# A four-layer graph network on one core: the first basis products of the next edge tile are issued ahead of the first half of a tile's messages

## The reference

```python
def _L1_gnn_ref(node_feat, edge_sh, edge_inv, edge_weight_cutoff, Wk1, ..., Wv3, W_logit, W_out, edge_src, edge_dst):
    x_src = node_feat[edge_src]
    def f(W1, W2, W3):
        tp = (x_src[:, :, None] * edge_sh[:, None, :]).reshape(n_edges, d * s)   # 64 features x 8 components
        out1 = jnp.concatenate([x_src, tp], axis=-1)                             # 576 columns
        out2 = _mlp(edge_inv, W1, W2, W3)
        return out1 * out2
    ...
    alpha = exp / z[edge_dst]                     # softmax weights over the edges of a destination, 4 heads
    edge_v = f(Wv1, Wv2, Wv3)
    edge_v = edge_v.reshape(n_edges, H, F // H) * jnp.sqrt(jax.nn.relu(alpha))[:, :, None]
    node_out = jax.ops.segment_sum(edge_v.reshape(n_edges, F), edge_dst, num_segments=n_nodes)
    return node_out @ W_out
```

## Time and profile before

| | us |
|---|---|
| median of 3 runs (lowest, highest) | 4221.5 (4217.95, 4222.28) |
| the profiled execution's own time | 4220.62 |
| its span in the trace | 4218.8 |
| DVE busy in the span | 3706.1 |
| PE busy in the span | 3078.8 |

### The profile page before, as it was taken

The page is one execution under the profiler, slowest core; times in us unless marked ns, Lnnn a source line. Parts: engine busy times, 40 slices in busy tenths (PEclk is TensorE's granted clock), DMA queues, the critical chain, the costliest instruction groups (busy, mean ns, idle before and its releaser), DMA issues. The chain is left out here.

```text
span 4218.8 us, 129416 instructions
## 1 busy us (share of the span) xinstructions
PE 3078.8 (73%) x53233; PEld 1918.5 (45%) x53233; DVE 3706.1 (88%) x5487; ACT 1777.2 (42%) x3388; POOL 1850.4 (44%) x3678
## 2 busy tenths in 40 slices
PE   5566556466388888888883699999999995166166
PEld 2111111212156566666662577777777774122122
DVE  8999999799778888888788888888888885898898
ACT  6999988477222232333231222222222221085086
POOL 0100455100376676777672466666666665000000
PEclk9889887677699999999997899999999997598599
DMA  4863899766255555555551233333333332554554
GB/s 162 307 269 147 301 362 353 264 205 210 71 139 143 138 152 146 145 148 147 149 144 54 66 103 102 102 103 104 103 101 102 103 104 83 190 198 181 190 182 175
DMA packets 412793, 680.07 MB, mean 161 GB/s; under 512 B 75244, under 2 KB 353068, under 8 KB 400560
## 3 DMA queue, kind: packets, MB, share of 16 engines
q1 hardware_dynamic: 336736, 559.22, 40.0%
q0 software_dynamic: 39568, 78.78, 6.9%
q10 hardware_dynamic: 35904, 33.79, 2.7%
HBM read 399.92 MB, written 271.65 MB: 159 GB/s over the span
## 5 line engine op out<-in xcount | busy, mean ns | idle before, releaser
L734 POOL DMA_INDIRECT arena<-h_table,srci x808 | 773.7, 958 | 315.5 <-issue 205.8
L830 PE MATMUL banks<-arena 128*128 128x500 bf16 x1440 | 428.8, 431 | 278.9 <-DVE arena L1496 219.7
L1901 DVE TENSOR_TENSOR arena<-banks,arena 128x1024 f32<-128x1024 f32 x404 | 492.0, 1218 | 100.7 <-PE banks L1046 95.1
L1787 DVE TENSOR_TENSOR arena<-banks,arena 128x1024 f32<-128x1024 f32 x404 | 491.8, 1217 | 68.5 <-PE banks L937 63.9
L1909 DVE TENSOR_TENSOR arena<-banks,arena 128x1024 f32<-128x1024 f32 x404 | 494.8, 1225 | 36.9 <-PE banks L1055 0.3
L1185 ACT ACTIVATE arena<-arena,h 128x128 bf16<-128x128 f16 x1440 | 454.5, 386 | 81.3 <-DVE arena L1509 41.4
L1055 PE MATMUL banks<-arena 64*64 64x256 f32 x6464 | 432.8, 383 | 50.0 <-DVE arena L1909 50.0
L948 PE MATMUL banks<-arena 64*64 64x128 f32 x12928 | 437.4, 274 | 0.0
L1074 PE MATMUL banks<-arena 64*64 64x128 f32 x12928 | 435.8, 272 | 0.3 <-DVE arena L1909 0.3
L1484 DVE TENSOR_SCALAR arena<-arena,agg 128x500 bf16<-128x500 f16 x1440 | 410.4, 345 | 0.2
L830 PEld LDWEIGHTS banks<-arena 128*128 128x128 bf16 x1440 | 126.6, 104 | 579.7 <-DVE arena L1484 438.8
(11 more groups left out here) (297 smaller groups left out, 5768.0 us busy)
## 6 DMA issues: line engine op xcount, KB each, us to landing
arena<-c_flat SPq DMA_DIRECT2D x75, 1562.5 KB, 6.8
slots<-arena SPq DMA_DIRECT2D x90, 1000.0 KB, 4.8
arena<-hs_dump SPq DMA_DIRECT2D x404, 128.0 KB
arena<-mask_rows SPq DMA_DIRECT2D x50, 781.2 KB, 4.3
arena<-in_edge_attr SPq DMA_DIRECT2D x202, 128.0 KB
arena<-placed SPq DMA_DIRECT2D x202, 128.0 KB
xs_dump<-arena SPq DMA_DIRECT2D x202, 128.0 KB
hs_dump<-arena SPq DMA_DIRECT2D x202, 128.0 KB
```

The source lines that it names most:

```text
L734: pool.indirect_dma_start(out=xs[par][:, k * D:(k + 1) * D], out_offset=None, in_=h_table, in_offset=bass.IndirectOffsetOnAxis(ap=srci[:, ...
L830: last = pe.matmul(ps[4 + r % 2][:, 0:BW], row_hot[r][:, k * P:(k + 1) * P], col_hot[r][:, k * BW:(k + 1) * BW], start=k == 0, stop=k == K ...
L1787: V.tensor_tensor(bt[h].rearrange("p (s n) -> p s n", s=4), banks[:, 4 * COLS:6 * COLS].rearrange("p (s n) -> p s n", s=4), h2k[t % 3].rea ...
L1901: V.tensor_tensor(dt_[h].rearrange("p (s n) -> p s n", s=4), banks[:, 0:2 * COLS].rearrange("p (s n) -> p s n", s=4), xat[t % 3].rearrange ...
```

## The change

PE's wait for the hidden features and basis rows and the first basis products move from the head of a tile to the middle of the tile before it, between the back transposes and the first half of the messages. Tile 0's are issued in the round before it. No instruction is added or removed, and no other engine's list differs.

```diff
@@ -1103,8 +1103,6 @@
             pe.wait_ge(wo_in, 16 * 2 * (S + 1))
             for t in range(-1, T + 1):
                 if 0 <= t < T:
-                    pe.wait_ge(hidden_in[t % 2], (t // 2 + 1) * 64)
-                    p2_basis(t, 0)
                     p2_value(t, 0)
                     p2_own(t)
                 if 0 <= t - 1:
@@ -1118,6 +1116,9 @@
                     p2_turned(t + 1)
                 if 0 <= t - 1:
                     p2_back(t - 1)
+                if t + 1 < T:
+                    pe.wait_ge(hidden_in[(t + 1) % 2], ((t + 1) // 2 + 1) * 64)
+                    p2_basis(t + 1, 0)
                 if 0 <= t < T:
                     at(msg_sb, t, pe)
                     pe.wait_ge(vt_sb, t * 3 + 1)
                     p2_message(0).then_inc(half_ps, 1)
```

## The result

The changed kernel takes 4167.8 us (median of 4 runs, 4156.8 to 4177.4), the kernel before 4221.9 (4 runs, 4218.0 to 4225.0). The ratio is 0.9872, with a 95% interval of 0.9844 to 0.9899. It is faster, as forecast, but by 54 us where 88 were forecast, and the time lies above the range. Its runs also spread over 20 us, where those before spread over 7. The profiled execution is the slowest of the four, 4177.4, with a span of 4175.6.

What follows compares the result with a forecast made beforehand. It took a ring of PE and DVE waiting in turn, 5.79 us a tile, as the bound. Falling to 5.35 saves 0.44 over 201 tiles, 88 us: 4221.5 - 88 = 4133, range 4118 to 4158.

Steps and rivals of the forecast that it cites:

- The old ring: In the second edge pass, PE and DVE wait in turn, 5.78 us a tile, with message 0 queued before basis 0.
- PE alone 5.33: PE's new order in the second edge pass, if it waited for nothing, would take 5.33 us a tile.
- ring through own: Values 1 on DVE to value 0 and own message on PE, back to own and values 1: 5.32 us a tile.
- PE is fuller than the starts say: Rival: PE alone needs 5.54 us a tile in the pass, gain 50 us, time 4171; chance 0.07.
- ring (c): Own on DVE waits for the previous tile's own message on PE; the next values 1 starts 4.04 us after value 0.
- own can start at V + 2.41: V is value 0's start on PE; own on DVE could start 2.41 us later, after the own message.
- The rivals on the loads: Late `hidden_in` loads hold PE before basis 0: 5.44 a tile, 4151, chance 0.05; or 6.04, 4272, chance 0.03.
- DVE alone, 5.21: Rival: own need not wait, so DVE's own work sets 5.21 us a tile, gain 117 us, 4105; chance 0.05.
- Not slower: Against the case of PE standing before basis 0 with message 0 behind it, 4272 us; chance of slower 0.03.
- the change does what it says: Against the rival that something other than basis 0's queue place holds DVE's 0.47 wait, 4221; chance 0.01.
- The sum: Second edge pass: 5.79 - 5.35 = 0.44 us saved a tile over 201 tiles, 88 us in all.
- The bounds of the step: Tile 5.30 us (4123) to 5.42 (4147), from hand-overs off by 0.05 or PE and DVE waiting in turn a little.

Runs made afterwards that it cites:

- e1: The changed kernel with a second buffer for the own block, so own on DVE no longer waits for the previous tile's own message; 4157.1 us, ratio 0.9836.
- e11: The changed kernel with one buffer, PE doing its own message ahead of message 1 and signalling DVE at once; 4141.8 us, ratio 0.9837.
- e3: The changed kernel with half as many message products, each twice as wide, so PE has the same time but fewer instructions; 4163.1 us, ratio 0.9846.
- e4: The changed kernel without loads of hidden features and basis rows after the first two tiles, whose data are reused; 4167.8 us, ratio 0.9859.
- e8: The changed kernel with two buffers for own and the store of running sums issued ahead of the loads; 4140.5 us, ratio 0.9817.
- e12: The changed kernel with two buffers for own, the store of running sums ahead of the loads, and basis rows loaded early; 4126.7 us, ratio 0.9792.
- e5: The changed kernel without the two loads of basis rows a tile after the first two tiles; 4176.9 us, ratio 0.9892.
- e6: The changed kernel without the two loads of hidden features a tile after the first two tiles; 4167.6 us, ratio 0.9870.
- e10: The changed kernel with one buffer for own and the store of running sums issued ahead of the loads; 4175.0 us, ratio 0.9912.

## Why the prediction was wrong, point by point

- **The old ring.** Right: it was closed by basis 0 behind message 0. DVE's 95.1 us and PE's 50.0 us went to 0.9 and 0.5, rows 0 follows values 1 after 1.14, and ACT's copy of the turned rows is in time.
- **PE alone 5.33.** The number came out: e1 and e11, with the ring through own open, run at 5.335. That it is PE alone is not shown. The 1.02 from value 1 to the transposes was taken from a group that had waited, and in e1 value 1 still starts 1.28 after values 0 and looks 0.05 longer, so the ring over values 0 described there may hold the tile. PE quite alone would then need some 5.28, an estimate: 5.335 less the 0.05. The rival "PE is fuller than the starts say" (5.54) is out. So is the reading of its busy share: 99% with a hidden wait in it at 5.46, and the tile still fell by 0.13.
- **The step that failed: ring (c), "own can start at V + 2.41".** It starts at V + 2.54 (2706.91 - 2704.37). Two terms were short. From value 0 to the own message are 2.00 and not 1.96, because a value group that waited for DVE runs 0.05 longer to the next group; the row from which 0.86 was taken had not waited, and the other value group of rows 5, which had, showed 1.09. In the changed kernel value 0 to own takes 0.91. And from the own message to DVE are 0.54 and not 0.45: the figure was borrowed from ACT's use of the same message (0.46 there) and from another group. With 0.01 more for own itself, the ring through own is 5.46 where 5.32 was worked out; e1 and e11, which open it, bring the tile to 5.335. It is a ring of one tile, closed by the 1.28 from values 1 to value 0. It was named, and its sum came out 0.14 short. That is 0.117 a tile (5.467) against the forecast of 5.35, over 201 tiles 23 us.
- **What was missing: the fetch of PE's instructions.** No term and no rival had it. It gave back most of the 18 us of the long tiles in the profiled execution: 23 times PE stood in a group until 1.2 to 1.6 us after an instruction packet had landed. The rivals on the loads looked at the same transfers, but at their landing: in e3 and e4 it is seen that they matter through the instruction queue and not through `hidden_in`, whose waits for a transfer come to 0.4 us in the changed kernel.
- **DVE alone, 5.21:** not reached in any run. By the rule of the Trainium skill (Perfetto Trace Analysis, Identifying the Most-Contended Engine) that was the place where the change would end; no run went under 5.33. What the same section says of the busy share of products, that it is no good measure of how close TensorE is to its limit, is borne out here: at 99% the tile could still fall by 0.13.
- **Not slower, the change does what it says:** both right.
- **The sum.** Forecast 88 us. The ring took 23 of it, the long tiles 18, the rest outside the pass 3: 88 - 23 - 18 - 3 = 44, against 43.3 in the profiled execution. The bounds of the step allowed the hand-overs to be off by 0.05 each and ended at 5.42 a tile (4147); the range went on to 4158 for the sake of the loads. The tile of 5.467 alone, without one long tile, gives 4157, inside by a microsecond. The long tiles put the time outside.

## What to carry to other kernels

When an operation is taken out of a ring between two engines, work out every ring that stays, also those in which the other engine waits, with hand-over times taken from the same pair of engines in the same state, waiting or not: where three rings lie within 0.03 us of each other, an error of 0.1 in one decides the result. A buffer that costs nothing before may be the next bound; opening the ring through own was worth another 0.13 us a tile here, and nothing at all without the first change. And an engine that is made to run without pause also uses up its instructions without pause. Gaps inside a group of instructions that wait for nothing, at the beat of the instruction queue, are to be looked for on the most densely issued engine.

## What was not expected of the hardware

- PE's instruction stream is brought by transfers of its own, one packet to about 250 products and weight loads. At 5.79 us a tile they were never late enough to leave a gap; at 5.46 and 5.33 PE ran dry 11 to 29 times in 201 tiles, unless the instructions were fewer (e3: never), the loads gone (e4: once), or the store first with two buffers (e8 and e12: 3 times). Every one of these gaps ended 1.2 to 1.6 us after such a packet had landed. How a load holds the fetch up was not found; e5, e6 and e10 show that it is neither bytes nor the number of issues alone, nor simply their order.
- PE's records can read 99% busy while PE waits twice a tile. The wait shows only in small things: 0.05 us more in the group's length, up to 0.07 more from the start of the group before, and a start that always lies the same 1.28 us behind DVE's.
- From the start of the same products to their first use took 0.47 us on ACT (2706.37 to the 2706.84 below) and 0.54 on DVE. ACT in the changed kernel:

```profile
2706.84 0.39 ACT L1338 ACTIVATE arena<-banks 128x256 f32<-128x256 f32 x1 [2.90 <-PE banks L1081]
```
